# Token mixing: gated products two tiles behind the gating, with six gated buffers

## The reference

```python
q = x @ Wq + bq
k = x @ Wk + bk
v = x @ Wv + bv
scores = jnp.einsum('btd,bsd->bts', q, k)
retained = jnp.einsum('bts,bsd->btd', d_gamma_batched * scores, v)
y = retained @ Wo + bo
out = jnp.where(y >= 0, y, prelu_a * y)
```

## Time and profile before

| what | value |
|---|---|
| median of 3 runs | 3947.42 us (3943.25 to 3950.13) |
| the profiled execution | 3942.37 us, span 3940.6 us |
| mean granted TensorE clock | 0.987 |
| busy in the span: PE, DVE, ACT, POOL | 95%, 80%, 61%, 2% |
| mixing, from the first x transposes to the last copy of xs | 30.9 to 421 us |
| encoder and what follows | 421 to 3940.6 us |

### The profile page before, as it was taken

The page is one execution under the profiler, slowest core; times in us unless marked ns, Lnnn a source line. Parts: engine busy times, 40 slices in busy tenths (PEclk is TensorE's granted clock), DMA queues, the critical chain, the costliest instruction groups (busy, mean ns, idle before and its releaser), DMA issues. The chain is left out here.

```text
span 3940.6 us, 159991 instructions
## 1 busy us (share of the span) xinstructions
PE 3751.8 (95%) x61932; PEld 2744.1 (70%) x61932; DVE 3135.7 (80%) x21227; ACT 2391.8 (61%) x11882; POOL 85.2 (2%) x129
## 2 busy tenths in 40 slices
PE   6899899999999999999999899999999999999998
PEld 3233688888888888888888666666666666666664
DVE  5888899999999999999998677667776667776675
ACT  3223688888888888888888334444434444444443
POOL 6100000000000000000000000000000000000000
PEclk8999999999999999999999999999999999999999
DMA  3010000000000000000000000000000000000000
GB/s 90 18 26 20 8 3 3 3 3 3 3 3 3 3 3 3 3 3 3 3 3 5 4 8 8 6 6 8 8 8 6 8 6 8 8 8 6 6 8 7
DMA packets 49571, 34.01 MB, mean 9 GB/s; under 512 B 37661, under 2 KB 46877, under 8 KB 48806
## 3 DMA queue, kind: packets, MB, share of 16 engines
q1 hardware_dynamic: 48806, 23.77, 2.3%
HBM read 15.37 MB, written 8.39 MB: 6 GB/s over the span
## 5 line engine op out<-in xcount | busy, mean ns | idle before, releaser
L731 PE MATMUL bank<-xs,ident 128*128 128x128 f16 x15583 | 1413.9, 222 | 0.0
L731 PEld LDWEIGHTS bank<-xs,ident 128*128 128x128 f16 x15583 | 1010.1, 102 | 252.3 <-issue 230.0
L751 ACT ACTIVATE ifg_cell_dec<-bank 128x48 f32<-128x48 f32 x1024 | 215.1, 210 | 640.4 <-PE bank L743 640.4
L743 PE MATMUL bank<-enc_lo,u_hi 128*128 128x16 f16 x8192 | 528.9, 173 | 0.3 <-DVE enc_lo L803 0.3
L740 PE MATMUL bank<-enc_hi,u_lo 128*128 128x16 f16 x8192 | 527.2, 172 | 0.0
L766 DVE SCALAR_TENSOR_TENSOR terms_dec<-ifg_cell_dec 128x32 f32<-128x32 f32 x1024 | 196.7, 192 | 397.9 <-ACT ifg_cell_dec L751 386.7
L740 PE MATMUL bank<-enc_hi,u_hi 128*128 128x16 f16 x8192 | 500.5, 169 | 0.0
L740 PEld LDWEIGHTS bank<-enc_hi,u_lo 128*128 128x128 f16 x8192 | 338.8, 96 | 206.4 <-DVE enc_hi L797 171.9
L758 ACT ACTIVATE bank<-twice_cell_dec 128x16 f32<-128x16 f32 x1024 | 191.7, 187 | 402.2 <-DVE twice_cell_dec L772 402.2
L743 PEld LDWEIGHTS bank<-enc_lo,u_hi 128*128 128x128 f16 x8192 | 338.6, 96 | 67.8 <-DVE enc_lo L803 0.4
L740 PE MATMUL bank<-ring_hi,u_lo 128*128 128x16 f16 x4096 | 260.4, 172 | 102.0 <-DVE ring_hi L797 95.5
(11 more groups left out here) (268 smaller groups left out, 7889.5 us busy)
## 6 DMA issues: line engine op xcount, KB each, us to landing
g_rows<-tok_d_gamma_batched_dram SPq DMA_DIRECT2D x8, 512.0 KB, 6.5
x_rows<-in_x_dram SPq DMA_DIRECT2D x16, 256.0 KB, 3.1
kept_h<-tok_ln_h SPq DMA_DIRECT2D x32, 128.0 KB, 2.1
res<-kept_h SPq DMA_DIRECT2D x32, 128.0 KB
out_dram<-sums SPq DMA_DIRECT2D x32, 128.0 KB
raw_wd<-in_L_attn_Wd_dram SPq DMA_DIRECT2D x2, 256.0 KB
raw_experts<-in_L_ffn_W_dram SPq DMA_DIRECT2D x2, 256.0 KB
raw_u<-in_L_attn_Uf_dram SPq DMA_DIRECT2D x1, 256.0 KB
```

The costliest lines, as they stand in the source:

```text
L731: nc.tensor.matmul(spare, m.ident16[:], m.xs[:, 0, :, :].rearrange("p b t -> p (b t)"), start=False, stop=True, skip_group_check=True)
L743: last = nc.tensor.matmul(z[k], m.u_hi[c.d][:, g, :], h_lo, start=False, stop=True, skip_group_check=True)
L751: nc.scalar.activation(c.ifg_cell[:, 0:3, :], ifg, ACT.Tanh, scale=1.0 / Z_SCALE).then_inc(c.s_t_ifg, 1)
```

## The change

The products move from two tiles at place n (those of n - 1 and n) to the pair n - 3 and n - 2; the last pair, of the last batch, is made by a new `flush` behind the last place. There are six gated buffers for four. Every step of `post` moves two places back (yT from 0 to 2, its transposes from 1 to 3, neg from 2 to 4, and so on); the norm's transposes move by one, from 12 to 13, and the copy to xs from 13 to 14. `prep` stays.

```diff
-    G_RING = 4
+    G_RING = 6
@@ batches
+            if flush:
+                flush()
             for t in range(NT):
                 post(B - 1, t)
@@ PE
+                def product_pair(n):
+                    pe.wait_ge(s_g, n + 2)
+                    product(*divmod(n, NT))
+                    product(*divmod(n + 1, NT))
+
                 def products(b, t):
 
-                    if t % 2:
-                        pe.wait_ge(s_g, NT * b + t + 1)
-                        product(b, t - 1)
-                        product(b, t)
+                    n = NT * b + t - 3
+                    if t % 2 and n >= 0:
+                        product_pair(n)
+
+                def last_products():
+                    product_pair(NT * B - 2)
@@ PE, post
-                    if t == 1:
+                    if t == 3:
                         pe.wait_ge(s_yT, b + 1)
-                    if t == 12:
+                    if t == 13:
                         pe.wait_ge(s_n, b + 1)
@@ ACT, post
-                    if t == 0:
+                    if t == 2:
                         act.wait_ge(s_av, NT * (b + 1))
-                    if t == 7:
+                    if t == 9:
                         act.wait_ge(s_var, b + 1)
-                    if t == 9:
+                    if t == 11:
                         act.wait_ge(s_nm, b + 1)
-                    if t == 13:
+                    if t == 14:
                         act.wait_ge(s_nT, b + 1)
@@ DVE, post
-                    if t == 2:
+                    if t == 4:
...
-                    if t == 10:
+                    if t == 12:
                         dve.wait_ge(s_nh, b + 1)
```

More of the change, by code:

```diff
@@ L415, in token_mixing, with batches @@
         DVE_TILE = {11: 0, 12: 1, 13: 2, 14: 3}
-        def batches(main, prep, post, finish=None):
+        def batches(main, prep, post, finish=None, flush=None):
             for b in range(B):
@@ L560, in _ @@
                 scores(0, 1)
-                batches(scores_ahead, prep, post, products)
+                batches(scores_ahead, prep, post, products, last_products)
             @block.scalar
@@ L637, in post @@
                     own = latest[0] if latest else None
-                    if t == 3:
+                    if t == 5:
                         own.wait()
@@ L642, in post @@
                             ).then_inc(s_h, 1)
-                    if t == 4:
+                    if t == 6:
                         dve.wait_ge(s_h, b + 1)
@@ L647, in post @@
                         own.made(TS(ln.mean[:], ln.total[:], 1.0 / D, None, ALU.mult))
-                    if t == 5:
+                    if t == 7:
                         own.wait()
                         own.made(TT(ln.centred[:], ln.h[:], over_tokens(ln.mean[:]), ALU.subtract))
-                    if t == 6:
+                    if t == 8:
                         own.wait()
                         own.made(TT(ln.square[:], ln.centred[:], ln.centred[:], ALU.mult))
-                    if t == 7:
+                    if t == 9:
                         own.wait()
@@ L658, in post @@
                         TS(ln.var[:], ln.squares[:], 1.0 / D, EPS, ALU.mult, ALU.add).then_inc(s_var, 1)
-                    if t == 8:
+                    if t == 10:
                         dve.wait_ge(s_sd, b + 1)
```

## The result

The changed kernel took 3924.3 us (median of 5 runs, 3918.03 to 3930.02) against 3947.42 of the kernel before (now 5 runs, 3943.25 to 3950.13; the median is that of the first 3). The ratio is 0.9940 with a 95% interval of 0.9928 to 0.9953: 23.1 us, 0.6% faster. Forecast were 3924.8 us and 22.6 us less.

What follows compares the result with a forecast made beforehand. PE, busy 20.66 of each 22.34 us mixing period, was taken as nearly the bound. Gains 20.2 + 3.3 - 0.9 = 22.6 us, from the median 3947.42, gave 3924.8 us; own range 3917 to 3932.

Steps and rivals of the forecast that it cites:

- The ring, and its 1.68 us: Change of batch in the mixing: waits through PE, ACT and DVE idle PE 0.49 and 1.19 us; removal gives 20.2 us.
- No wait of PE is left; margins of 0.5 to 0.9: Steady batch in the new order: inputs come 0.5 to 0.9 us before PE needs them, so the period is 20.66 us.
- yT's margin: ACT's copy of the values in a steady batch: done at 2.8 us, PE comes at 3.3, 0.5 us to spare.
- Rival 1: DVE's norm chain comes 0.9 us late to place 13: period 21.55 us, gain 9.5, time 3938 us; chance 0.09.
- Neg's new wait: DVE's neg, due at 3.3 us in a steady batch, waits 0.75 us for the turned values at 4.0.
- Six buffers cost nothing: Gating n on DVE waits for product n-6, issued by place n-3, ahead of its own scores: no cost.
- The gap ahead of products: PE between scores and products: the 0.10 us ahead of a pair stays, despite early gatings.
- Rival 4: The 0.10 us ahead of 8 pairs in 13 batches goes too: 10 us more gain, 3915 us; chance 0.05.
- The first batches, 3.3 us: Batch 2, beside POOL's work: square still ends at 114.06, PE then needs 5.3 us, so batch 3 starts 3.3 us earlier.
- The last batch, 0.9 us lost: Last batch, paced by DVE: place 0 to last product takes 18.7 us instead of 17.84, costing 0.9.
- Rival 2: Nothing moves: with three score banks PE waits at the scores for the same gating; 3947 us, chance 0.06.
- rival 3: yT slips behind xs and x_split in ACT's queue, holding PE at place 3: period 23.16, 3957 us; chance 0.04.

## Why the prediction was right, point by point

- *The ring, and its 1.68 us.* Right in place and cause: ACT's order alone removes one stand, undoing it in the changed kernel makes one of 2.66. Its size was too small. I took the idle columns, 0.49 and 1.19; the period fell by 22.34 - 20.45 = 1.89. The busy time of 20.66 contained the tails of records: a matmul is shown for 0.38 us where the next starts after 0.22, and this tail is counted as busy even where nothing follows. By starts the pair of 211.70 could have begun at 211.15, 0.31 behind the last scores (210.84), and that of 215.44 at 214.13, 0.53 behind the yT transposes (213.60), as both do after the change. The two stands are thus 0.55 and 1.31, together 1.86 us. Twelve periods gave 22.7 us, not 20.2.
- *No wait of PE is left; margins of 0.5 to 0.9.* Right: idle 0.0 ahead of products and scores. yT's margin was put at 0.5, and in the rows ACT ends it at 207.04 and PE comes at 207.53. Rival 1 did not come about. Neg's new wait was put at 0.75 and is 0.62.
- *Six buffers cost nothing.* Right, and needed; but the release of a first product, which the sum did not use, I would have had too early by 0.6 us.
- *The gap ahead of products.* It stayed: the last scores start at 204.89, the products at 205.20, 0.31 us later. The row held. The rule of the Trainium skill ("TensorE: Matmul & The Clock Gate", Part 2, Step-by-step) that weight loads are pulled ahead of matmuls in flight did not show itself for these f32 products: their loads start with them, not before, although their gatings had ended over 1 us earlier. Rival 4 is out.

```profile
205.19 0.20 PEld L489 LDWEIGHTS bank<-gated,vo 128*64 128x64 f32 x4 [0.42 <-issue]
```

- *The first batches, 3.3 us.* This is the step that failed, by size. Its main claim held closely: the norm's last square, at 110.10 for 3.96 us before, now starts at 110.33 for 3.95 and ends at 114.28 against 114.06. In both kernels it ends 0.55 us behind the same POOL instruction (L331 on the rows of the biases, which ends at 113.51 before and 113.73 after), and q_lo follows at once. DVE was further ahead in its queue and only waited longer (L677, 4.20 us at 105.89). But PE then needed 7.5 us for what I had put at 5.3, place 0 of batch 3 came at 122.43 instead of 120.05, and the gain was 0.9 us. The rows of PE show why:

```profile
110.18 0.61 PE L476 MATMUL bank<-q_hi,k_both 128*128 128x512 f16 x1 [6.48 <-DVE gated L632]
110.58 0.63 PE L476 MATMUL bank<-q_lo,k_both 128*128 128x512 f16 x1
114.94 0.61 PE L562 MATMUL bank<-ones_s,bias 128*128 128x512 bf16 x1 [3.73 <-DVE q_lo L704]
115.34 0.64 PE L563 MATMUL bank<-xT,wq_hi 128*128 128x512 f16 x1
...
118.76 0.64 PE L564 MATMUL bank<-xT,wk_lo 128*128 128x512 f16 x1
```

  After stands of 6.48 and 3.73 us the steps are 0.43 us apart instead of 0.22: the granted clock is at its lower level, 1.2 GHz, from 105.9 to 119.6. In the kernel before it was there from 106.7 to 113.5 only, its stands in this stretch being 2.50 and 2.08 us, and the work behind the square went at full clock (118.00 to 118.22 for one step). I priced the new order from those rows. But in the new order PE stands longer before q_lo comes, and the clock comes back 6.1 us later: 2.2 us more for the same matmuls. The step that failed is thus the price of PE's work behind the square, 7.5 us for 5.3.
- *The last batch, 0.9 us lost.* Place 0 at 122.43 + 12 x 20.45 = 367.8, the last product done at 386.03: 18.2 us against 17.84, a loss of 0.4. With these, 22.7 + 0.9 - 0.4 = 23.2 us, what the end of the mixing shows. Two errors of 2.5 and 2.4 us had opposite signs: that the total came within 0.6 us is luck, while the mechanism of the largest term is not.
- *Rival 2 and rival 3.* Out. The run with ACT's order undone is near to rival 3: slower, by work queued around yT on ACT. But there x_split stands behind yT, not yT behind x_split, and PE stands ahead of the scores of place 2, not ahead of yT's transposes.

## What to carry to other kernels

When a wait closes a ring over several in-order queues, look at which unrelated instruction stands behind the waiting one in each queue: here a ready one (x_split) behind a late one (yT) on an engine that is busy a third of the time held up PE. Deferring a consumer makes its last result later, so look at what is queued behind that result on other engines, and move it too: with yT left at place 0 the same deferral went with a slower kernel. Where a helper engine holds up another, try shorter instructions before less work. And when a new order makes an engine stand longer, do not price the work behind the stand with the rows of the old order.

## What the runs showed that I had not expected

- The two products of a pair (f32, 128x64 weights on 512 columns, into the two halves of a bank's partitions) go side by side. In the changed kernel the four records of the pair at 205.20 start at 205.196, 205.202, 205.677 and 205.682 us; a view that ends 0.4 us behind the start shows two of them, together lasting 0.65 us, and all four last 1.08. The counter of products goes up at 206.283 and 206.326. Who waits for the first is let go only 0.04 us before who waits for the second.
- A DVE step that met one of POOL's instructions on the rows of the biases (3x1608) was held until that instruction ended, although POOL touched three partitions only. In the changed kernel the square was held for 3.95 us at 110.33, and a step of only 8 columns (L677) for 4.20 us at 105.89, beside POOL's L330 from 105.73 to 110.07. Not every step is held: the gating at 97.70, which reads its scores from PSUM, took 0.68 us inside POOL's L328 (97.12 to 101.97). With pieces of 201 columns the slowest step in batch 3 was 0.99 us, at 109.50.
- Equal stands do not cost the same. With ACT's order undone, PE stands 2.66 us in every period, and from 199.5 us on, behind every second stand, the granted clock is at its lower level for 3.4 us, which costs 1.43 us more.
- The runs of the kernel with small POOL instructions spread over 2.1 us (4 runs), those of the changed kernel over 12.0 us (5 runs) and those of the kernel before over 6.9 us. Why was not looked into; the low clock after PE's long stands is one candidate.
